# A 64-byte first write into the output, placed at the head of the store queue, in a conditioned matrix product with residual

## The chip, the cores and the metric

The kernel runs on one core of one Trainium2 chip. The metric is the device time of one execution in microseconds (us), as the median of several runs. Kernel before: 320.21 us, median of 3 runs (320.0 to 321.37).

## What is computed

For each of 64 batches a 128x128 weight matrix is picked out of 16 by the batch's condition, the transposed matrix is multiplied with the batch's 128x2048 block of x, and x is added. All of it is float32.

```
x: (64, 128, 2048), condition: (64,) integers 0 to 15, weights: (16, 128, 128)
W = weights[condition]
return x + jnp.einsum('bct,bcd->bdt', x, W)
```

## The kernel before

The host lays x out as 16 groups of four batches. A group is a block of 128 rows (one per channel, one per SBUF partition) by 8192 columns: 32 KiB in each row, 4 MiB in all. The output has the same layout.

`x_ring` in SBUF has four rooms, each as large as one group. Each queue does one job:

- SP (L53 to L60) issues one DMA for each group, `x_ring<-x`, 16 in all. The first four go out at once. The load of group g from the fifth on (L57) waits until the store of group g-4 has landed, since it goes to the same room.
- ACT (L105 to L124) issues, in this order, the load of `weight_table` (all 16 matrices, 128 rows of 8 KiB, 1 MiB), the load of `condition_row` (256 bytes in one row), one store of 4 MiB for each of the groups 0 to 14 when the last of the group's four sums is done (L113), and four stores of 1 MiB for group 15 (L121), each when its sum is done.
- POOL (L63 to L74) waits for `condition_row` and `weight_table` (L67, L68), and then for each batch reads the condition and copies the chosen 128x128 matrix to `chosen_weights` (L73). Sixteen such buffers exist, so the copies run far ahead.
- PE (L77 to L91) waits at each group for its load and at each batch for the chosen matrix and for a free half of PSUM (`product` holds two batches), and issues four matmuls 128x512 (L88) for each batch.
- DVE (L94 to L102) adds the product to the tile in `x_ring`, in place (L101), one operation of 128x2048 for each batch.

So the order of work is a ring: load, four batches on PE, sum, store, and the room is free for the next load. No order is planned elsewhere: the two DMA queues (SP's, q1 in the profile, for the loads of x; ACT's, q10, for everything else) each keep the order in which they were issued, and both feed the same 16 DMA engines. PE can't begin before the table and the conditions have landed, and both of them stand at the head of the queue that later carries the stores.

Of the kernel before, what the change touches and what calls it, by code (L numbers as in the profile page):

```python
# [1 line left out]

# [3 lines left out]

BANK_COLUMNS = 512
PSUM_BANKS = 8
GROUP = 4
ROOMS = 4  # L10


def conditioned_residual(nc, x, condition, weights, out):
    fp32 = mybir.dt.float32
    groups, channels, group_columns = x.shape
    batches = groups * GROUP
    time = group_columns // GROUP
    _, states, features = weights.shape
    matmuls = time // BANK_COLUMNS
    psum_slots = PSUM_BANKS // matmuls  # L20
    per_turn = ROOMS * GROUP
    turns = batches // per_turn

    with ExitStack() as ctx:
        def sbuf(name, shape, dtype=fp32):
            return ctx.enter_context(nc.sbuf_tensor(name, shape, dtype))

        def sem(name):
            return ctx.enter_context(nc.semaphore(name))

        x_ring = sbuf("x_ring", [channels, ROOMS * group_columns])
        weight_table = sbuf("weight_table", [channels, states * features])
        chosen_weights = [sbuf(f"chosen_weights{b}", [channels, features]) for b in range(per_turn)]
        condition_row = sbuf("condition_row", [1, batches], condition.dtype)
        product = ctx.enter_context(nc.psum_tensor("product", [features, psum_slots, time], fp32))

        condition_loaded = sem("condition_loaded")
        table_loaded = sem("table_loaded")
        x_loaded = [sem(f"x_loaded{g}") for g in range(ROOMS)]
        room_stored = [sem(f"room_stored{r}") for r in range(ROOMS)]  # L40

        weights_chosen = [sem(f"weights_chosen{b}") for b in range(per_turn)]
        product_done = [sem(f"product_done{b}") for b in range(per_turn)]
        sum_done = [sem(f"sum_done{b}") for b in range(per_turn)]

        def sums_wanted(turn, b):
            return turn + (2 if b >= per_turn - psum_slots else 1)

        block = ctx.enter_context(nc.Block())

        @block.sync  # L53
        def _(sp):
            for g in range(groups):
                room = g % ROOMS
                if g >= ROOMS:  # L57
                    sp.wait_ge(room_stored[room], 16 * (g // ROOMS))
                sp.dma_start(x_ring[:, room * group_columns:(room + 1) * group_columns], x[g]
                             ).then_inc(x_loaded[g % ROOMS], 16)  # L60

        @block.gpsimd
        def _(pool):  # L63
            for b in range(per_turn):
                pool.sem_inc(product_done[b], 1)
            pool.wait_ge(condition_loaded, 16)
            pool.wait_ge(table_loaded, 16)  # L67
            with pool.Fori(0, turns) as turn:  # L68
                for b in range(per_turn):
                    state = pool.value_load(condition_row[0:1, bass.ds(turn * per_turn + b, 1)],  # L70
                                            min_val=0, max_val=states - 1)
                    pool.wait_ge(product_done[b], turn + 1)  # L72
                    pool.tensor_copy(chosen_weights[b][:, :],  # L73
                                     weight_table[:, bass.ds(state * features, features)]  # L74
                                     ).then_inc(weights_chosen[b], 1)

        @block.tensor  # L77
        def _(pe):
            for b in range(per_turn - psum_slots, per_turn):
                pe.sem_inc(sum_done[b], 1)  # L80
            with pe.Fori(0, turns) as turn:
                for b in range(per_turn):
                    if b % GROUP == 0:
                        pe.wait_ge(x_loaded[b // GROUP], 16 * (turn + 1))
                    pe.wait_ge(weights_chosen[b], turn + 1)
                    pe.wait_ge(sum_done[(b - psum_slots) % per_turn], turn + 1)
                    for m in range(matmuls):
                        last = pe.matmul(  # L88
                            product[:, b % psum_slots, m * BANK_COLUMNS:(m + 1) * BANK_COLUMNS],
                            chosen_weights[b][:, :],  # L90
                            x_ring[:, bass.ds(b * time + m * BANK_COLUMNS, BANK_COLUMNS)],  # L91
                            start=True, stop=True)
                    last.then_inc(product_done[b], 1)

        @block.vector
        def _(dve):
            with dve.Fori(0, turns) as turn:
                for b in range(per_turn):
                    tile = x_ring[:, bass.ds(b * time, time)]
                    dve.wait_ge(product_done[b], turn + 2)  # L100
                    dve.tensor_tensor(tile, product[:, b % psum_slots, :], tile,  # L101
                                      AluOpType.add).then_inc(sum_done[b], 1)  # L102

        @block.scalar
        def _(act):  # L105
            act.dma_start(weight_table[:, :], weights.rearrange("c s d -> c (s d)")  # L106
                          ).then_inc(table_loaded, 16)
            act.dma_start(condition_row[0:1, :], condition.rearrange("(o b) -> o b", o=1)
                          ).then_inc(condition_loaded, 16)
            for g in range(groups - 1):  # L110
                room, last = g % ROOMS, (g % ROOMS + 1) * GROUP - 1
                act.wait_ge(sum_done[last], sums_wanted(g // ROOMS, last))
                act.dma_start(out[g], x_ring[:, room * group_columns:(room + 1) * group_columns]  # L113
                              ).then_inc(room_stored[room], 16)

            g = groups - 1
            for i in range(GROUP):
                b = (g % ROOMS) * GROUP + i
                column = (g % ROOMS) * group_columns + i * time
                act.wait_ge(sum_done[b], sums_wanted(g // ROOMS, b))  # L120
                act.dma_start(out[g, :, i * time:(i + 1) * time], x_ring[:, column:column + time]  # L121
                              ).then_inc(room_stored[g % ROOMS], 16)
            for r in range(ROOMS):
                act.wait_ge(room_stored[r], 16 * (groups // ROOMS + (GROUP - 1 if r == g % ROOMS else 0)))  # L124


# [20 lines left out]
```

## Time and profile before

| | us |
|---|---|
| median of 3 runs | 320.21 |
| profiled execution, its own time | 320.21 |
| its span, first to last instruction | 318.4 |
| PE busy | 249.3 (78%) |
| DVE busy | 146.7 (46%) |
| POOL busy | 19.2 (6%) |
| DMA, mean over the span | 425 GB/s |

The span leaves out 1.8 us before the first and after the last instruction. The page cuts the span in 40 slices and tells for each how busy the DMA engines were; the chain of waits follows the last work back to the start. "DMA to landing" is the time from the issue of a DMA to the moment when its last semaphore increment arrived. In views by windows the DMA share is the mean busy share of the 16 DMA engines; since packets are booked as wholes, it can pass 1 in a short window.

### The profile page before, as it was taken

How to read it: one execution, taken by the hardware profiler on the slowest of the kernel's cores; microseconds unless marked ns; L12 is line 12 of the kernel's file. 1: busy time of each engine (PE TensorE's matmuls, PEld its weight loads, DVE VectorE, ACT ScalarE, POOL GpSimd, SP SyncE). 2: the span in 40 equal slices, each digit the busy share in tenths (PEclk: the TensorE clock that was granted, in tenths of full speed). 3: DMA queues.
4: the chain of work that ended last, by engine and by line, in shares of the span. 5: the costliest groups of instructions: out<-in, count | busy, mean ns of one | idle time of the engine just before them, and what ended most of it. 6: DMA issues, size and time to landing. Idle time of an engine off the chain costs nothing.

```text
span 318.4 us, 1662 instructions
## 1 busy us (share of the span) xinstructions
PE 249.3 (78%) x512; PEld 106.1 (33%) x512; DVE 146.7 (46%) x64; POOL 19.2 (6%) x69
## 2 busy tenths in 40 slices
PE   0069999995996969779597895959969598796960
PEld 0024444442432424334243341424424243342420
DVE  0006766765262553717337262551626537165460
POOL 0023101000010000000000000000000000000000
PEclk9999999999796998979789798996979979598996
DMA  8999999999999999999999999999999999999997
GB/s 313 428 445 433 424 395 440 416 457 399 461 424 432 436 420 457 416 445 424 430 445 412 457 424 432 436 420 457 399 461 428 428 436 420 457 416 445 424 406 297
DMA packets 5188, 135.29 MB, mean 425 GB/s; under 512 B 578, under 2 KB 578, under 8 KB 578
## 3 DMA queue, kind: packets, MB, share of 16 engines
q10 hardware_dynamic: 2882, 68.16, 49.7%
q1 hardware_dynamic: 2304, 67.11, 49.3%
q8 instruction: 1, 0.02, 0.0%
q14 instruction: 1, 0.01, 0.0%
HBM read 68.16 MB, written 67.11 MB: 425 GB/s over the span
## 4 chain that ended last, share of the span: by engine, by line
DMA 61%; PE 33%; DVE 3%; POOLq 0%; issue 0%; ACTq 0%; POOL 0%
PE product L88 33%; DMA out<-x_ring 30%; DMA x_ring<-x 25%; DMA condition_row<-condition 5%; DVE x_ring L101 3%; POOLq L70 0%; ACTq L106 0%; POOL chosen_weights L73 0%; POOLq L68 0%; POOLq L73 0%; POOLq L72 0%
## 5 line engine op out<-in xcount | busy, mean ns | idle before, releaser
L88 PE MATMUL product<-x_ring,chosen_weights 128*128 128x512 f32 x512 | 249.3, 651 | 58.5 <-DMA x_ring<-x 39.5
L101 DVE TENSOR_TENSOR x_ring<-product,x_ring 128x2048 f32<-128x2048 f32 x64 | 146.7, 2292 | 163.5 <-PE product L88 163.5
L88 PEld LDWEIGHTS product<-x_ring,chosen_weights 128*128 128x128 f32 x512 | 106.1, 210 | 201.0 <-issue 151.5
L73 POOL COPY chosen_weights<-weight_table 128x128 f32 x64 | 18.9, 296 | 212.6 <-PE product L88 185.3
L132 POOL MEMSET const-float32-0.0<- 128x1 f32 x1 | 0.1, 99 | 0.1
L132 POOL MEMSET const-bfloat16-1.0<- 128x1 bf16 x1 | 0.1, 102 | 0.0
L132 POOL MEMSET const-uint8-127<- 128x1 uint8 x1 | 0.1, 102 | 0.0
L132 POOL MEMSET const-float32-1.0<- 128x1 f32 x1 | 0.1, 99 | 0.0
L132 POOL BASE_LOAD x1 | 0.0, 17 | 0.1
## 6 DMA issues: line engine op xcount, KB each, us to landing
x_ring<-x SPq DMA_DIRECT2D x16, 4096.0 KB, 26.7
out<-x_ring ACTq DMA_DIRECT2D x15, 4096.0 KB, 31.6
out<-x_ring ACTq DMA_DIRECT2D x4, 1024.0 KB, 9.2
weight_table<-weights ACTq DMA_DIRECT2D x1, 1024.0 KB, 15.0
condition_row<-condition ACTq DMA_DIRECT2D x1, 0.2 KB
```

The source lines that it names most:

```text
L73: pool.tensor_copy(chosen_weights[b][:, :], weight_table[:, bass.ds(state * features, features)]).then_inc(weights_chosen[b], 1)
L88: last = pe.matmul(product[:, b % psum_slots, m * BANK_COLUMNS:(m + 1) * BANK_COLUMNS], chosen_weights[b][:, :], x_ring[:, bass.ds(b * tim ...
L101: dve.tensor_tensor(tile, product[:, b % psum_slots, :], tile, AluOpType.add).then_inc(sum_done[b], 1)
L132: nc = bacc.Bacc("TRN2", target_bir_lowering=False, num_devices=1)
```

## The change

A tile `first_write` of 128x16 float32 is added. DVE sets it to zero before its loop. ACT, as its first act, waits for that, and writes the tile to the first 16 columns of group 0 in `out`: 128 rows of 64 bytes. Only then it issues the loads of `weight_table` and `condition_row`. Before the loop over the groups it waits until the 64-byte rows have landed, so that the store of group 0, which writes the same places, can't be overtaken by them. Nothing else differs; the output is the same, as group 0's store writes over the zeros.

```diff
+FIRST_WRITE = 16
...
+        first_write = sbuf("first_write", [channels, FIRST_WRITE])
...
+        first_write_ready = sem("first_write_ready")
+        first_write_done = sem("first_write_done")
...
         @block.vector
         def _(dve):
+            dve.memset(first_write[:, :], 0).then_inc(first_write_ready, 1)
             with dve.Fori(0, turns) as turn:
...
         @block.scalar
         def _(act):
+            act.wait_ge(first_write_ready, 1)
+            act.dma_start(out[0, :, 0:FIRST_WRITE], first_write[:, :]).then_inc(first_write_done, 16)
             act.dma_start(weight_table[:, :], weights.rearrange("c s d -> c (s d)")
                           ).then_inc(table_loaded, 16)
             act.dma_start(condition_row[0:1, :], condition.rearrange("(o b) -> o b", o=1)
                           ).then_inc(condition_loaded, 16)
+            act.wait_ge(first_write_done, 16)
             for g in range(groups - 1):
```

## Rows read from the trace of the kernel before

**Rows 1.** The page: busy time by engine, and DMA in 40 slices.
```profile
PE 249.3 (78%) x512; PEld 106.1 (33%) x512; DVE 146.7 (46%) x64; POOL 19.2 (6%) x69
...
DMA  8999999999999999999999999999999999999997
GB/s 313 428 445 433 424 395 440 416 457 399 461 424 432 436 420 457 416 445 424 430 445 412 457 424 432 436 420 457 399 461 428 428 436 420 457 416 445 424 406 297
```

**Rows 2.** Stretches: us; busy PE, PEld, DVE, POOL (count); PE clock; DMA share; GB/s.
```profile
0.00:1.70 1.70, 0.00 (x0) 0.00 (x0) 0.00 (x0) 0.22 (x5) 1.00 0.00 0
1.70:3.70 2.00, 0.00 (x0) 0.00 (x0) 0.00 (x0) 0.00 (x0) 1.00 0.94 266
...
38.20:43.00 4.80, 4.80 (x12) 2.09 (x11) 3.66 (x2) 0.59 (x2) 1.00 0.96 341
43.00:53.00 10.00, 10.00 (x25) 4.40 (x24) 6.58 (x4) 0.89 (x3) 1.00 0.99 426
60.00:290.00 230.00, 192.75 (x389) 81.22 (x388) 111.37 (x50) 10.95 (x37) 0.89 1.00 433
```

**Rows 3.** Chain that ended last, in order of time, its beginning: start, us, what.
```profile
0.79 0.40 ACTq L106
1.19 0.03 issue
1.22 16.16 DMA condition_row<-condition
...
18.99 56.90 PE product L88 x128
```

**Rows 4.** Timeline of DMA issues and of POOL's memsets, 0 to 2 us.
```profile
0.40 0.10 POOL L132 MEMSET const-uint8-127<- 128x1 uint8 x1
0.79 0.40 ACTq L106 DMA_DIRECT2D weight_table<-weights  x1
0.79 1.32 SPq L59 DMA_DIRECT2D x_ring<-x  x3
1.22 0.54 ACTq L108 DMA_DIRECT2D condition_row<-condition  x1
```

**Rows 5.** The page: DMA issues by line, KB each, us to landing (median).
```profile
x_ring<-x SPq DMA_DIRECT2D x16, 4096.0 KB, 26.7
out<-x_ring ACTq DMA_DIRECT2D x15, 4096.0 KB, 31.6
out<-x_ring ACTq DMA_DIRECT2D x4, 1024.0 KB, 9.2
weight_table<-weights ACTq DMA_DIRECT2D x1, 1024.0 KB, 15.0
```

**Rows 6.** Loads of x (L59) issued at 0.79 (first) and 1.22 us (second).
```profile
DMA to landing us min/median/max: 14.8/14.8/14.8
...
DMA to landing us min/median/max: 24.1/24.1/24.1
```

**Rows 7.** Timeline of the first stores (ACT queue, from 30 us on).
```profile
37.04 14.08 ACTq L113 DMA_DIRECT2D out<-x_ring  x2
```

**Rows 8.** Group 0's store (L113), issued at 37.04 us: its landing.
```profile
DMA to landing us min/median/max: 18.1/18.1/18.1
```

**Rows 9.** Timeline of SP's DMAs from 50 us, and landing of the first (L59, group 4).
```profile
55.20 16.03 SPq L59 DMA_DIRECT2D x_ring<-x  x2
...
DMA to landing us min/median/max: 24.0/24.0/24.0
```

**Rows 10.** Timeline of PE: runs of matmuls [idle before <-releaser], three of twelve stalls.
```profile
79.26 15.70 PE L88 MATMUL product<-x_ring,chosen_weights 128*128 128x512 f32 x32 [3.38 <-DMA x_ring<-x]
98.62 16.84 PE L88 MATMUL product<-x_ring,chosen_weights 128*128 128x512 f32 x32 [3.66 <-DMA x_ring<-x]
...
292.27 15.59 PE L88 MATMUL product<-x_ring,chosen_weights 128*128 128x512 f32 x32 [2.63 <-DMA x_ring<-x]
```

**Rows 11.** Timeline of DVE, first two sums.
```profile
24.41 2.29 DVE L101 TENSOR_TENSOR x_ring<-product,x_ring 128x2048 f32<-128x2048 f32 x1 [24.41 <-PE product L88]
27.85 2.29 DVE L101 TENSOR_TENSOR x_ring<-product,x_ring 128x2048 f32<-128x2048 f32 x1 [1.14 <-PE product L88]
```

## The prediction

> **What bounds the kernel now.** I read the busy times first, then the DMA slices, the chain of waits, and last the landings of single DMAs. PE is busy 78% of the span and DVE 46%, while the DMA engines show nine tenths or more in every slice but the first and the last [rows 1]. From 60 to 290 us their share is 1.00 at 433 GB/s, and PE stalls before each group for its load, 3.38 us at 79.26 and 2.63 us at 292.27, in all twelve times [rows 2, 10]. So the bytes set the pace. Whatever keeps the 16 DMA engines idle is added to the end, and whatever PE loses is free as long as both queues still hold work.
>
> One row of a group is 32 KiB, and 128 rows over 16 engines are 8 rows for each. At 433 GB/s [rows 2] the 16 engines move one such row each in 16 x 32768 B / 433 GB/s = 1.21 us; call that a turn. A load or store of 4 MiB alone is 8 turns, 9.7 us; a row of the table, 8 KiB, is 0.30 us.
>
> How the two queues share the engines decides this case, and the landings tell it. The table and group 0 of x are issued together at 0.79 us [rows 4]. The table is a quarter of the bytes, yet it takes 15.0 us to land and group 0 takes 14.8 [rows 5, 6]. If bytes were shared evenly the table would be there after twice 1 MiB, 5 us and a start. If the queues take turns row by row, both end after 8 x (1.21 + 0.30) = 12.1 us plus the start. The start is 1.0 us from issue to first data (nothing moves before 1.7 us) and a slow first row (2.0 us at 266 instead of 433 GB/s, 0.8 us lost) [rows 2]: 13.9 us, and 14.8 to 15.0 with the spread of the engines. So **it is row by row, however short a row is**. `condition_row`, one row of 256 bytes right behind the table, lands at 17.38 us [rows 3], 1.6 us behind the table's 15.8: a tiny row waits for its turn too. The second load lands at 1.22 + 24.1 = 25.3 us, 9.7 us after the first [rows 6].
>
> **The change, part by part.**
>
> *Memset and ACT's first wait.* The nearest rows are POOL's memsets of 0.10 us [rows 4]. A memset of 128x16 and one semaphore between engines come to an estimated 0.2 us (ends: 0.1 and 0.5). SP doesn't wait for it, so group 0's load is issued first, where before both queues began together.
>
> *Eight 64-byte rows per engine at the head of ACT's queue.* Their own time is bounded by nothing at all below and by a table row, 0.30 us, above: 0 to 8 x 0.30 = 2.4 us. By bytes they are 1/128 of a table row; `condition_row` shows no cost besides its turn. I take 0.1 us. The Trainium skill (DMA: Bandwidth & Descriptors, Specifications) says that below 512 bytes the engine does a read-modify-write, which speaks for more; the trace before has only short reads, no short write of data, so no run here shows it yet.
>
> *What they delay.* Between any two of them stands a row of x. The table's rows, which before were paired with group 0's, are now paired with group 1's, and the conditions come 8 turns later: 8 x 1.21 = 9.7 us. Added to that is how far SP is ahead. A queue that joins late finds rows already taken on by the engines: group 4's load, issued at 55.20, lands after 24.0 us [rows 9], of which 16 alternating turns are 19.4, the start 1.0 and the spread some 0.9; about 2.7 us are left, two turns. At the start of the kernel before nobody was ahead. Now SP leads by 0.2 us, and I take two turns, 2.4 us (ends: none and two). The conditions thus land 9.7 + 2.4 + 0.1 = 12.2 us later, at 29.6 instead of 17.38, and PE begins at about 31.2 instead of 18.99 [rows 3].
>
> *What covers it, and where the cover ends.* Meanwhile the loads of groups 0 to 3 go on, so PE's late start costs nothing until they are through. Without a store beside them they land at 25.3 + 2 x 9.7 = 44.7 us. No fifth load can go out, all rooms are full. The first store was issued at 37.04 us [rows 7]; before that stand a start of PE and four batches, the sums 3.44 us apart [rows 11], all moved alike. It is now issued at 37.04 + 12.2 = 49.2, and its data start 1.0 us later, at 50.2. **The engines stand idle for 50.2 - 44.7 = 5.5 us**, where before the store came 7.7 us ahead of 44.7.
>
> *A second hole.* The store of group 0 now has the engines alone: 9.7 us, to about 60. Group 4's load waits for it; before it was issued 0.06 us after the landing (37.04 + 18.1 = 55.14 against 55.20) [rows 7, 8, 9]. Group 1's store comes four batches after the first, 49.2 + 13.7 = 62.9. So at 60 both queues are empty: 0.1 + 1.0 us until the load's first data, and a slow first row as at the start, 0.8 us [rows 2]. Together 1.9 us. Before, group 1's store filled this place.
>
> *Afterwards* nothing more is lost. Group 4's load is in at about 78 us, while PE is at groups 2 and 3 until some 88; from group 5 on both queues alternate as before, 19.4 us for each group against PE's 15.6 to 16.8. In the last 25 us the stores alone carry the work, in both kernels.
>
> *What it takes away.* Around the first store the rate falls: 341 GB/s from 38.2 to 43.0 us, against 433 later [rows 2]. That is 4.8 x (1 - 341/433) = 1.0 us lost, and it comes once. If it is a cost of the first write to the output, the early write pays it at the start, perhaps beside other waiting. I take the full 1.0 us as gained (ends: 0 and 1.0).
>
> *ACT's second wait* (for the 64-byte rows) costs nothing: they land before the table does, and ACT would wait for group 0's sums until past 37 us anyway. Nothing is queued behind it but the stores.
>
> Sum, against the profiled execution's own 320.21 us, which is also the median: 5.5 + 1.9 + 0.1 - 1.0 = +6.5 us, **326.7 us**. The ends: no turns lost by the lead (-2.4) gives 324.3; the 1.0 us not gained and dear short rows (+2.3) give 330.0.
>
> **Rivals.**
>
> *The short rows slip through* (ends on the other side). If all that stands in one queue back to back passes in one turn, or if turns count bytes, the 64-byte rows cost some 0.1 us and the table is 0.3 us later, the first store still comes well before 44.7 us, no hole opens, and the early write saves up to 1.0 us: 319.3 to 320.3. It decides as soon as the conditions land less than about 6.7 us later (44.7 - 37.04 - 1.0), for until then the loads cover all. For it: the trace has no stretch with 64-byte rows. Against it: the table's landing level with group 0's, and the turn that `condition_row` had to wait. The Trainium skill (DMA: Bandwidth & Descriptors, Queues, rings and completion order) has such a rule: an engine drains a whole packet, typically 9 to 17 descriptors, from one ring before it switches. Applied to the table and the conditions before, it would have landed them together, where 1.6 us lie between; the trace disagrees. Chance 0.09.
>
> *The short rows are dear.* If each 64-byte write holds its engine longer than a table row, 0.3 us or more, 8 of them move everything by over 2.4 us, loads included: from 329.1 us up, with 0.4 us each 329.8. For it: a write of part of a block is a kind of work not seen before. Against: 4 MiB stores run at the loads' rate. Chance 0.07.
>
> *It doesn't do what it says*: the dip around the first store stays since it belongs to the start of large stores, not to the first bytes. Then 327.7 us, within the forecast's own case.
>
> **How the numbers follow.** Turn by turn, with the lead at none to two turns and the dip gone or not, has 0.84: 324.3 to 327.7 us, likeliest 326.7. The range reaches from 323.5 (a hole smaller than worked out, PE's start being a little faster) to 330.0, and takes in most of the dear rows; the slipping rows stay out. A measurement of this kernel can tell some 0.5%, 1.6 us, from no change. Slower by more than that is everything but the slipping rows, and a bit of doubt: 0.91. Within 0.5%: 0.07. Faster by more would need twice the dip's 1.0 us: 0.02.
>
> **What would show it.** The conditions landing near 29.6 us in the chain of waits, and PE beginning near 31; group 0's load landing earlier, near 13 us, without the table beside it, and the table level with group 1's; a slice with DMA well below nine tenths between 44 and 50 us, and a smaller dip near 61; the first store landing about 11 us after its issue instead of 18.1; the last groups unchanged but for a shift. Wrong it is if the conditions land before 24 us, or if the holes are there and the end doesn't move with them.

## The result and the profile after

The changed kernel takes 328.61 us (median of 5 runs, 327.62 to 329.0) where the kernel before, run beside it, takes 320.42 us (320.0 to 321.37): a ratio of 1.025, 95% interval 1.0235 to 1.0266. It is slower by 8.2 us. The forecast was 326.7 us, in a range of 323.5 to 330.0.

The profiled execution of the changed kernel took 329.0 us with a span of 327.2, so 8.8 us more than the 318.4 before. The page of the changed kernel, busy times and DMA in 40 slices, to be set beside [rows 1]:

```profile
PE 248.6 (76%) x512; PEld 106.0 (32%) x512; DVE 146.8 (45%) x65; POOL 19.0 (6%) x69
...
DMA  8999928899999999999999999999999999999997
GB/s 321 408 448 427 450 128 385 320 381 449 445 397 437 449 441 413 429 449 441 417 423 445 445 417 425 445 445 429 409 449 445 429 417 441 445 449 397 441 414 307
```

One slice stands out, the sixth, from 40.9 to 49.1 us, with 128 GB/s; the seventh and eighth are lower as well. Everything behind them reads as before. The same part by stretches, first of the changed kernel (columns as in [rows 2]):

```profile
44.40:50.30 5.90, 5.90 (x15) 2.58 (x14) 3.84 (x2) 0.51 (x2) 1.00 0.00 0
50.30:60.20 9.90, 9.90 (x25) 4.37 (x24) 6.88 (x3) 0.88 (x3) 1.00 0.99 424
60.20:61.50 1.30, 1.30 (x5) 0.58 (x4) 0.68 (x1) 0.29 (x1) 1.00 0.00 0
...
63.80:68.60 4.80, 4.80 (x12) 2.11 (x12) 3.20 (x2) 0.59 (x2) 1.00 0.96 348
...
40.00:60.00 20.00, 20.00 (x48) 8.93 (x47) 13.75 (x6) 2.94 (x10) 1.00 0.67 288
60.00:80.00 20.00, 20.00 (x48) 8.80 (x47) 13.47 (x6) 1.76 (x6) 1.00 0.93 370
```

and of the kernel before:

```profile
40.00:60.00 20.00, 20.00 (x48) 8.90 (x47) 13.15 (x7) 1.78 (x6) 1.00 1.00 419
60.00:80.00 20.00, 16.62 (x39) 7.16 (x39) 12.50 (x6) 1.48 (x5) 1.00 1.01 437
```

For 5.9 us, and again for 1.3 us, not a byte moves. In bytes, 40 to 60 us lost 20 x (419 - 288) / 433 = 6.1 us of full work, and 60 to 80 us lost 20 x (437 - 370) / 433 = 3.1 us. That is 9.2 us, of which 80 to 100 us gives back a little: the 8.8 us of the span. So the whole loss lies between 40 and 80 us.

Who is late is told by the chain of waits of the changed kernel, whose start answers to [rows 3]:

```profile
0.89 0.05 DVE first_write L101
...
0.97 0.38 ACTq L114
...
1.37 0.45 ACTq L115
...
1.86 26.73 DMA condition_row<-condition
```

The conditions land at 1.86 + 26.73 = 28.59 us, 11.2 us later than before. The page's DMA issues of the changed kernel, beside [rows 5]:

```profile
x_ring<-x SPq DMA_DIRECT2D x16, 4096.0 KB, 28.3
out<-x_ring ACTq DMA_DIRECT2D x15, 4096.0 KB, 29.9
out<-x_ring ACTq DMA_DIRECT2D x4, 1024.0 KB, 7.8
weight_table<-weights ACTq DMA_DIRECT2D x1, 1024.0 KB, 25.2
out<-first_write ACTq DMA_DIRECT2D x1, 8.0 KB, 13.4
```

8 KB took 13.4 us to land, at 14.4 us, and the table behind them 25.2 us. Group 0's load landed at 0.79 + 12.4 = 13.2 us instead of 15.6 [rows 6], since its rows now alternated with rows of 64 bytes instead of 8 KiB. ACT's first store is issued at 49.48 us:

```profile
49.48 253.04 ACTq L123 DMA_DIRECT2D out<-x_ring  x15
```

### The profile page after: what moved, and what is told of

Its sections match the earlier page's. It is cut to its first block, busy times and chain, and to the rows that moved or that the text cites. A ratio compares the mean times of both kernels' runs of the same rounds, so it can differ in the third digit from the quotient of the medians.

```text
span 327.2 us, 1665 instructions
## 1 busy us (share of the span) xinstructions
PE 248.6 (76%) x512; PEld 106.0 (32%) x512; DVE 146.8 (45%) x65; POOL 19.0 (6%) x69
## 4 chain that ended last, share of the span: by engine, by line
DMA 61%; PE 32%; DVE 3%; POOLq 0%; issue 0%; ACTq 0%; POOL 0%; DVEq 0%
PE product L92 32%; DMA out<-x_ring 27%; DMA x_ring<-x 26%; DMA condition_row<-condition 8%; DVE x_ring L106 3%; POOLq L74 0%; ACTq L115 0%; ACTq L114 0%; POOL chosen_weights L77 0%; POOLq L72 0%; POOLq L77 0%; DVE first_write L101 0%; POOLq L76 0%; DVEq L102 0%
## 6 DMA issues: line engine op xcount, KB each, us to landing
weight_table<-weights ACTq DMA_DIRECT2D x1, 1024.0 KB, 25.2
out<-first_write ACTq DMA_DIRECT2D x1, 8.0 KB, 13.4
```

## The experiments

Every edit is made to the changed kernel, unless the text says that it is made to the kernel before. Two theories stood against each other. **Turns:** whatever stands ahead of the table in ACT's queue costs the table one turn (1.21 us, a 32 KiB row of x) for each row and engine, whatever its size or direction; the end moves when the first store comes too late for the loads to cover it. **First write:** there is something about writes, be it a price of short ones, or a gain by paying the dip of [rows 2] (341 GB/s around the first store) early.

**The early write behind the table and the conditions.**

```diff
-            act.wait_ge(first_write_ready, 1)
-            act.dma_start(out[0, :, 0:FIRST_WRITE], first_write[:, :]).then_inc(first_write_done, 16)
             act.dma_start(weight_table[:, :], ...
             act.dma_start(condition_row[0:1, :], ...
+            act.wait_ge(first_write_ready, 1)
+            act.dma_start(out[0, :, 0:FIRST_WRITE], first_write[:, :]).then_inc(first_write_done, 16)
             act.wait_ge(first_write_done, 16)
```

> The same 64-byte write, but issued behind the loads of the table and the conditions. Turns theory (each row ahead of the table costs it one turn of 1.21 us, and the idle DMA engines between the last free load and the first store make the loss): the conditions land at 17.4 us as before, no hole opens, 320.2 to 320.7 us; and since the changed kernel's dip only moved to where a store joins running loads, the dip stays between 38 and 43 us at about 341 GB/s. Theory of the first write (the dip is the price of the first bytes written to the output, and can be paid early): the dip is gone, 319.2 to 319.5 us.

Measured: 320.45 us against 320.30, ratio 1.0006 (0.9997 to 1.0015). The chain shows the conditions at 1.22 + 16.17 = 17.39 us. So the loss hangs on the place in the queue. And the dip is there still, a little later because the first store was issued at 37.99 us:

```profile
1.22 16.17 DMA condition_row<-condition
```

```profile
39.20:44.00 4.80, 4.80 (x13) 2.10 (x12) 3.66 (x2) 0.56 (x2) 1.00 0.99 362
```

An early first write that nothing waits behind neither costs nor saves anything here. The dip isn't the price of the first bytes written.

**One row for each engine instead of eight.**

```diff
-            act.dma_start(out[0, :, 0:FIRST_WRITE], first_write[:, :]).then_inc(first_write_done, 16)
+            act.dma_start(out[0, 0:16, 0:FIRST_WRITE], first_write[0:16, :]).then_inc(first_write_done, 16)
```

> The early write cut to 16 rows, one for each DMA engine, at the same place at the head of the queue. Turns theory: besides the row only its semaphore entry and SP's lead delay the table, so the conditions land about 3 turns later (21 us instead of 28.59), the first store is issued at 41 to 42 us, before the loads run out at 44; no first hole, at most the second one after the first store's landing: 321.0 to 322.3 us. If what costs is having an early write at all, whatever its number of rows: about 328.6 us.

Measured: 323.11 us, ratio 1.0089 (1.0075 to 1.0102). The conditions are at 1.86 + 19.84 = 21.70 us, as expected, but the time is 0.8 us above the expected range. Two stretches of this kernel show why, beside the second hole that was expected:

```profile
43.00:48.00 5.00, 5.00 (x13) 2.25 (x12) 3.12 (x2) 0.59 (x2) 1.00 0.96 354
...
54.90:56.20 1.30, 1.30 (x4) 0.57 (x3) 1.30 (x1) 0.00 (x0) 1.00 0.00 0
...
57.50:62.50 5.00, 5.00 (x13) 2.16 (x12) 3.86 (x2) 0.59 (x2) 1.00 0.89 328
```

There are **two dips**, one at each of the first two stores. Group 0's store had landed, at 55.3 us, before group 1's was issued at 56.4, so the ACT queue started from empty twice while a load was running. In the kernel before it starts so once, as group 1's store queues up behind group 0's.

This run also corrects the prediction on where the cover ends. I had written that the loads cover all until the conditions come 6.7 us later; here they come 4.3 us later, there is no first hole, and still 2.8 us are lost. The second hole has an earlier limit of its own: group 0's store lands near 55 us whether it starts at 37 or at 43, since the engines have the same bytes to move until then, and group 1's store comes 13.7 us after the first. An estimate from these rows: once the first store is issued later than 55.3 - 1.0 - 13.7 = 40.6 us, both queues are empty for a while.

**A read in place of the write.**

```diff
-            act.dma_start(out[0, :, 0:FIRST_WRITE], first_write[:, :]).then_inc(first_write_done, 16)
+            act.dma_start(first_write[:, :], x[0, :, 0:FIRST_WRITE]).then_inc(first_write_done, 16)
```

> The same 128 rows of 64 bytes at the same place, but read from x into the tile instead of written to the output (the output is as before, nothing is left out). Turns theory: direction doesn't matter, conditions at 28.6 us, 328 to 329 us. If short writes are dear, by a read-modify-write or a wait for the write's receipt: well below, 320 to 326 us.

Measured: 328.61 us, ratio 1.0269 (1.0252 to 1.0285), the median of the change (that the hundredths agree is chance, since each kernel's executions spread over more than 1 us). The conditions land at 1.86 + 26.71 = 28.57 us against 28.59:

```profile
1.86 26.71 DMA condition_row<-condition
```

Direction makes no difference that the time can show, and 64-byte writes aren't dearer than 64-byte reads here.

**No early write; the table in two halves.** The edit is made to the kernel before; POOL waits for both halves.

```diff
-            act.dma_start(weight_table[:, :], weights.rearrange("c s d -> c (s d)")
-                          ).then_inc(table_loaded, 16)
+            half = states * features // 2
+            for h in range(2):
+                act.dma_start(weight_table[:, h * half:(h + 1) * half],
+                              weights.rearrange("c s d -> c (s d)")[:, h * half:(h + 1) * half]
+                              ).then_inc(table_loaded, 16)
...
-            pool.wait_ge(table_loaded, 16)
+            pool.wait_ge(table_loaded, 32)
```

> The kernel before with no early write; the table is loaded as two DMAs of 128 rows of 4 KiB, so 8 more rows (and one more semaphore entry) for each engine and not a byte more. Turns theory: the conditions land 8 to 9 turns later, at 27 to 28 us, the first store at 47 to 48.5, a hole of 4 to 5.5 us from 44 us and the second one after the first store: 326.3 to 328.0 us. If bytes or writes were what delays: 320.2 to 320.7 us.

Measured: 327.59 us, ratio 1.0236 (1.0217 to 1.0255). The same bytes in 16 rows for each engine instead of 8 cost nearly what the change costs. Chain, then the hole by stretches:

```profile
1.71 25.86 DMA condition_row<-condition
```

```profile
44.40:48.60 4.20, 4.20 (x11) 1.83 (x10) 2.29 (x1) 0.29 (x1) 1.00 0.02 8
```

There is no write, no new tile, no memset and no wait on ACT in this kernel, and yet the same hole opens: in these 4.2 us only one row's worth of bytes is moved. So neither bytes nor writes delay the conditions. The run alone doesn't tell whether a turn is one row or all that a DMA has on an engine, as the table is now two DMAs; the runs with one and with four rows tell that (below).

**The memset and ACT's wait without the early write.**

```diff
-            act.dma_start(out[0, :, 0:FIRST_WRITE], first_write[:, :]).then_inc(first_write_done, 16)
...
-            act.wait_ge(first_write_done, 16)
```

> The memset and ACT's wait for it stay, the early write itself is left out; so the table is issued 0.2 us after group 0's load and nothing stands ahead of it. It measures SP's lead alone. Turns theory: one turn (1.2 us) for the lead, conditions at 18.6 us, no hole, 320.2 to 321.5 us. If the lead were what makes the loss: 325 us or more.

Measured: 321.06 us, ratio 1.002 (1.0005 to 1.0035). The conditions land at 1.38 + 17.27 = 18.65 us, 1.27 us later than before, although the table was issued only 0.18 us later (0.97 instead of 0.79):

```profile
1.38 17.27 DMA condition_row<-condition
```

The lead of SP is worth one turn here, not two. The time moves by 0.6 us (0.2 to 1.1 by the interval), although the loads still cover the first store, issued at 38.12 us. The executions spread from 319.99 to 321.88 us; the profiled one took 320.25 and so shows no loss to read a cause from. What makes the slower ones stays open.

**Four rows for each engine.** The edit is that of the one row, with 64 in place of 16.

> The early write with 64 rows, four for each engine, between the one row (323.1 us) and the eight rows (328.6). Turns theory: conditions 3 turns later than with one row, at 25 to 25.5 us, the first store at 46 to 47, a first hole of about 2.5 us, and the second one: 323.9 to 326.0 us. A fixed cost of the write would give the 323.1 or the 328.6 of the neighbours.

Measured: 324.88 us, ratio 1.0147 (1.0123 to 1.0172), within the range. The conditions came at 2.19 + 23.02 = 25.21 us as expected, but the first store at 44.61, earlier than the 46 to 47, and the first hole is 1.4 us instead of 2.5. PE had a quick start in this execution (below).

```profile
44.10:45.50 1.40, 1.40 (x5) 0.61 (x4) 0.42 (x1) 0.00 (x0) 1.00 0.05 23
```

**The table and the conditions at the head of SP's queue,** the early write as in the change.

```diff
         def _(sp):
+            sp.dma_start(weight_table[:, :], weights.rearrange("c s d -> c (s d)")
+                          ).then_inc(table_loaded, 16)
+            sp.dma_start(condition_row[0:1, :], condition.rearrange("(o b) -> o b", o=1)
+                          ).then_inc(condition_loaded, 16)
             for g in range(groups):
...
-            act.dma_start(weight_table[:, :], weights.rearrange("c s d -> c (s d)")
-                          ).then_inc(table_loaded, 16)
-            act.dma_start(condition_row[0:1, :], condition.rearrange("(o b) -> o b", o=1)
-                          ).then_inc(condition_loaded, 16)
```

> The early write with all its 128 rows at the head of ACT's queue as in the change, but the table and the conditions are issued on SP's queue ahead of group 0's load, so that nothing PE waits for stands behind the early write. Turns theory: the loss is gone, conditions at 6 to 7 us, PE begins when group 0 has landed at 15 to 16 us, first store at about 34, no hole, 319.8 to 320.8 us. If an early write to the output costs in itself: about 328 us.

Measured: 320.33 us, ratio 1.0 (0.9988 to 1.0012). The early write stands where the change has it, and it costs nothing, since nothing that PE needs is behind it. PE begins at 16.16 us with group 0's landing, and the dip is at its place again, behind a first store issued at 35.19:

```profile
36.20:41.00 4.80, 4.80 (x12) 2.12 (x12) 3.62 (x2) 0.59 (x2) 1.00 1.00 355
```

**The same without the early write** (the memset, the tile, both waits and the 64-byte rows left out).

> As the run before it, without the early write: the kernel before with table and conditions at the head of SP's queue. PE begins some 3 us earlier than before, but the bytes set the pace, so 319.8 to 320.8 us, and equal to the run before it within 0.3 us if the early write is free where nothing stands behind it. If instead the first store's dip were paid early by the early write, that run would be 1.0 us faster than this one.

Measured: 320.38 us, ratio 0.9999 (0.999 to 1.0009): equal to the run before it, and to the kernel before. PE begins at 15.35 us, 3.6 us earlier than before, and wins nothing by it. No version that I ran beats the kernel before; with the DMA engines at 433 GB/s from 60 to 290 us [rows 2], none of these edits had more to win than the dip and the start.

The runs side by side. "Rows of x" are those that the engine which carries the conditions moved before their last entry. The records of single packets carry no engine number; I put them in order by joining each packet to the one that ended when it began. "Turns" is the difference to the kernel before.

| rows of 64 B for each engine | rows of x | turns | conditions land | first store issued | time (profiled execution) |
|---|---|---|---|---|---|
| none, and no wait (before) | 10 | 0 | 17.38 | 37.04 | 320.4 (320.21) |
| none, with the wait | 11 | 1 | 18.65 | 38.12 | 321.06 (320.25) |
| 1 | 13 | 3 | 21.70 | 42.69 | 323.11 (323.5) |
| 4 | 16 | 6 | 25.21 | 44.61 | 324.88 (324.22) |
| none, the table in 16 rows | 18 | 8 | 27.57 | 47.72 | 327.59 (327.21) |
| 8 (the change) | 19 | 9 | 28.59 | 49.48 | 328.61 (329.0) |

The turns are the early rows, one semaphore entry behind them (4 bytes, and it takes a turn as a row does), and SP's lead; one comes off where a semaphore entry of SP's own, after every eight rows of x, stands in place of a row. With eight rows that is 8 + 1 + 1 - 1 = 9, with one 1 + 1 + 1 = 3, with the halved table 8 + 1 - 1 = 8. With four it is 4 + 1 + 2 - 1 = 6: in that execution the lead was two rows of x. ACT took 0.56 us to issue the early write instead of 0.38, and from 4.5 to 6.0 us the changed kernel moves 16 short rows beside 16 long ones, the kernel with four rows none (first the changed kernel):

```profile
DMA packets 32, 0.53 MB, mean 350 GB/s; under 512 B 16, under 2 KB 16, under 8 KB 16
```

```profile
DMA packets 16, 0.52 MB, mean 350 GB/s; under 512 B 0, under 2 KB 0, under 8 KB 0
```

So the step from one row to four, 3.51 us, and the step from four to eight, 3.38 us, are three turns each. One, four and eight rows in one DMA cost 4.3, 7.8 and 11.2 us: a turn is one row and not one DMA.

## Why the prediction was right, and by how much it was off

**Row-by-row turns** held. The conditions were forecast at 29.6 us and came at 28.59. The rule of the Trainium skill that I had weighed against it (DMA: Bandwidth & Descriptors, Queues, rings and completion order: a whole packet of typically 9 to 17 descriptors is drained before a switch) would let 8 short rows and the table share their turns. If a packet takes in all that one DMA has on an engine, then one, four or eight short rows would cost the conditions the same. They cost 4.3, 7.8 and 11.2 us, and in the packet records short rows and rows of x alternate one for one; the trace disagrees. The halved table, 27.57 - 17.38 = 10.2 us for 8 more rows of half the size, fits the turns but wouldn't decide by itself. In these runs the row is the unit.

**The lead** was mis-sized: two turns forecast, one measured (18.65 against 17.38 us with the wait alone, and one in the changed kernel's packet records; two only in the execution with four rows). The two turns came from the landing of group 4's load, which joined a store in full flow; at the start of the program, one row had mostly been taken on. It made the forecast 1.2 us too long. The forecast also left out the early write's semaphore entry, one turn more, and SP's entry, one turn less; that they cancel is luck.

**PE's start** was taken as a constant, and isn't: that cancelled the lead's error, which is luck too. From PE's first matmul to the first sum it took 24.41 - 18.99 = 5.42 us before [rows 11]. In the changed kernel, by the timelines of PE and of DVE:

```profile
30.20 71.79 PE L92 MATMUL product<-x_ring,chosen_weights 128*128 128x512 f32 x160 [30.20 <-POOL chosen_weights L77]
```

```profile
36.79 2.29 DVE L106 TENSOR_TENSOR x_ring<-product,x_ring 128x2048 f32<-128x2048 f32 x1 [35.86 <-PE product L92]
```

That is 6.59 us, 1.17 us more, for the same four matmuls. The profile books each of them as two records (512 for the 256 of the kernel), and the records say where the time goes. First the kernel before, from 18.9 to 22.4 us, then the changed one, from 30.2 to 35.9 (count; shortest, median and longest in ns):

```profile
L88 PE MATMUL product<-x_ring,chosen_weights x4: 981/1061/1191, 19.0 to 21.7; 128*128 128x512 f32 x4
```

```profile
L92 PE MATMUL product<-x_ring,chosen_weights x7: 881/1061/1190, 30.2 to 35.4; 128*128 128x512 f32 x7
```

The records behind these take 592 ns. The slow records begin 0.86 us apart and the later ones 0.43, so PE starts at half its pace, the ratio of the two clock levels, 1.2 and 2.4 GHz, and leaves it after 4 records in one execution and after 7 in the other. The profile's clock row reads 1.00 in both, so it doesn't show this; what sets the moment stays open. The first sum came 6.71 us after PE's start with one early row and 5.11 with four, which is why that pair's first stores don't stand in step with their conditions. Hence the first store at 49.48 us where 49.2 was forecast, by two errors of opposite sign.

What PE's start is worth at the end can be read from the run with the reads, whose conditions land with those of the change (28.57 and 28.59 us). In its profiled execution the first sum comes 5.22 us after PE's start, the first store is issued at 48.08, 1.40 us earlier than in the change, and it took 327.77 us where the change's took 329.0, 1.2 us less.

**The first hole** was forecast from 44.7 to 50.2 us, 5.5 us; not a byte moves from 44.4 to 50.3. Right, short by 0.4 us. **The second hole** was forecast as 1.1 us empty and 0.8 us for a slow first row; it is empty for 1.3 us, from 60.2 to 61.5. The slow first row held: the 16 rows that begin at 61.6 take 2.0 us on average instead of 1.21, 0.8 us more, as at the program's start. These are the times in which no engine moves anything. Since the engines don't stop and start together, one engine is idle for 6.3 and 1.5 us on average (by the packet records). With the 0.8 us that is 8.6 of the 8.8 us of the profiled execution.

**The dip** is the step that failed: "I take the full 1.0 us as gained". It was not gained. It moved from group 0's store, which in the changed kernel has the engines alone, to group 1's, which joins group 4's load: 348 GB/s from 63.8 to 68.6 us, 4.8 x (1 - 348/433) = 0.9 us. So the term should have been near nothing, where it stood at -1.0 us. Putting it back gives 326.7 + 1.0 = 327.7 us, and 0.4 us for the first hole and 0.2 for the second make 328.3, against 328.61 measured. My rival for that case, "it doesn't do what it says", had named the value 327.7.

**Short rows** cost next to nothing of their own, as taken: reads and writes of 64 bytes give the same 328.61 us, and in the packet records each takes 0.011 us. The sentence of the Trainium skill on read-modify-write below 512 bytes (DMA: Bandwidth & Descriptors, Specifications) doesn't show in any time here. That they were writes changed nothing. The rivals of slipping and of dear rows both fall. But the slipping rival's limit, that the loads cover a delay of up to 6.7 us, was wrong for the turns too: 4.3 us of delay already cost 2.8 us in the run with one row, through the second hole and a second dip.

**Afterwards** the ring ran as forecast, 432 to 433 GB/s. What was said of ACT's second wait held also: the early rows landed at 14.4 us, the first store came at 49.48.

## What to carry to other kernels

Where two DMA queues feed the same engines and one carries long rows, the other gets one row in each turn, however short: count the rows (and semaphore entries) ahead of what an engine waits for, not the bytes. A small transfer belongs behind the loads that start the pipeline, or the loads that start it belong on the queue whose rows are long. And a late start of a hidden engine is free only as long as the buffers let the bound resource go on. Here that ended in two steps. A second hole, behind group 0's store, was there with the first store at 42.69 us and not with it at 38.12. The first hole opens when the loads of all four rooms are in, at 44.4 us, and from there the delay comes out whole: from four rows to eight the first store is issued 4.87 us later and the profiled executions are 4.8 us longer.

## What the hardware showed that I had not expected

- Where the store queue started from empty while a load was running, about 1 us of transfer was lost once, in each such place shown here: 341 GB/s over 4.8 us in the kernel before, 362 with the early write behind the table, 354 and 328 in the two dips with one row, 348 in the change. A store that has the engines alone shows none (424 GB/s from 50.3 to 60.2 us). In the kernel before it is the load that is slow: 30 rows of x, two for each engine, take 1.65 us on average instead of 1.21. But an empty queue is not the whole condition. In the profiled execution with the wait alone, group 2's store was issued at 65.59 us while group 1's was still under way (until 71.4), and a dip followed there as well:

```profile
66.60:71.40 4.80, 4.80 (x13) 2.17 (x12) 3.56 (x2) 0.59 (x2) 1.00 0.95 362
```

  The kernel before has none behind its third store (430 GB/s from 65.5 to 70.3 us). What the loss consists of stays open; the runs exclude only that it is the first write to the output.
- PE's first four matmuls take between 5.11 and 6.71 us to the first sum in the ten profiled executions, since PE runs its first 4 to 7 records at half pace under a clock row that reads 1.00. Where the first store decides, this alone moves it by 1.6 us. The pair of the change and the run with the reads, 1.4 us apart in the first store and 1.2 in the time, makes it the likely cause of the spread of the changed kernel's runs (327.62 to 329.0); only profiled executions show it, and each kernel has one.
- A difference of 0.18 us in the issue of a transfer cost 1.27 us at its landing, because the other queue was one long row ahead; with four rows, ACT was 0.18 us slower still, and one more turn was gone.
